# A graph-attention and feed-forward kernel: turned rows by DMA from chunk 3 on, with two sets of rows in memory and their loads ahead of x, output and s1

## What is computed

```python
def gnn(input1, input2, adj, a1, a2):
    e = input1 @ a1 + (input2 @ a2).T            # s1 of the row, s2 of the column
    e = jnp.where(e > 0, e, 0.2 * e)
    att = softmax(jnp.where(adj > 0, e, -9e15), axis=1)
    att = att * jnp.sum(adj, axis=1, keepdims=True)
    att = 0.1 * att + 0.9 * adj
    return att @ input2

x = x + gnn(layernorm(x), input2, adj, a1, a2)
x = x + layernorm(x) @ weight.T + bias
```

## Time and profile before

| | us |
|---|---|
| runs, median of 3 (lowest to highest) | 378.52 (377.69 to 378.69) |
| the profiled execution, its own time | 376.63 |
| its span, first to last instruction | 374.8 |
| PE busy in the span | 357.4 |
| PE weight loads busy | 313.6 |
| DVE busy | 311.4 |
| ACT busy | 252.9 |
| POOL busy | 146.6 |
| 4 loads of turned rows per chunk, 32 KB each: median from issue to landing | 11.8 |
| load of adj, 4 per chunk, 512 KB each: median from issue to landing | 10.9 |
| s1 into all partitions, 128 KB: median from issue to landing | 7.4 |
| x, 128 KB: median from issue to landing | 5.1 |

### The profile page before, as it was taken

The page is one execution under the profiler, slowest core; times in us unless marked ns, Lnnn a source line. Parts: engine busy times, 40 slices in busy tenths (PEclk is TensorE's granted clock), DMA queues, the critical chain, the costliest instruction groups (busy, mean ns, idle before and its releaser), DMA issues.

```text
span 374.8 us, 8950 instructions
## 1 busy us (share of the span) xinstructions
PE 357.4 (95%) x3199; PEld 313.6 (84%) x3199; DVE 311.4 (83%) x787; ACT 252.9 (67%) x616; POOL 146.6 (39%) x258
## 2 busy tenths in 40 slices
PE   5689999999999799999999999999999999999992
PEld 5578888888888688888888888888888888888881
DVE  5998989969999768879788888989687887999832
ACT  5799896697588568392947749294874929897100
POOL 4594713805262532608043260806225160703111
PEclk9999999999999999999999999999999999999998
DMA  7999959492959596694929487591958830121000
GB/s 251 202 214 202 218 110 183 78 192 45 171 119 174 117 144 136 81 202 89 204 45 181 91 145 139 96 199 42 160 118 117 160 72 2 32 26 44 30 18 30
DMA packets 34646, 45.72 MB, mean 122 GB/s; under 512 B 18084, under 2 KB 25896, under 8 KB 34600
## 3 DMA queue, kind: packets, MB, share of 16 engines
q0 software_dynamic: 9216, 33.56, 47.0%
q1 hardware_dynamic: 25384, 11.56, 16.4%
HBM read 74.84 MB, written 3.82 MB: 210 GB/s over the span
## 4 chain that ended last, share of the span: by engine, by line
PE 77%; DMA 8%; issue 5%; DVE 3%; POOL 2%; ACT 2%; SPq 1%; POOLq 0%; DVEq 0%
PE acc_u L760 23%; PE acc_v L763 23%; PE acc_y L742 21%; PE acc_v L742 4%; DMA adj_all<-adj 4%; PE acc_u L742 3%; DMA late<-block_rows 3%; PE acc_y L731 2%; PE small L725 2%; ACT steep L554 2%; DMA s_rows<-pre_s 1%; DVE plus L972 1%; POOL adj_all L409 1%; SPq L330 1%; PE acc_u L731 0%
## 5 line engine op out<-in xcount | busy, mean ns | idle before, releaser
L554 ACT ACTIVATE steep<-s_bc,steep_s 128x256 bf16<-128x256 f32 x512 | 218.2, 524 | 13.1 <-DMA s_bc<-s_rows 6.6
L763 PE MATMUL acc_v<-weights_v,minus 128*128 128x258 f16 x896 | 198.1, 272 | 0.0
L760 PE MATMUL acc_u<-weights_u,plus 128*128 128x258 f16 x896 | 198.1, 273 | 0.0
L742 PE MATMUL acc_y<-weights_y,adj_all 128*128 128x257 f16 x896 | 101.3, 273 | 0.4 <-DMA adj_all<-adj 0.4
L742 PEld LDWEIGHTS acc_y<-weights_y,adj_all 128*128 128x128 bf16 x896 | 86.8, 97 | 12.5 <-DMA adj_all<-adj 0.7
L760 PEld LDWEIGHTS acc_u<-weights_u,plus 128*128 128x128 bf16 x896 | 86.7, 97 | 12.0
L763 PEld LDWEIGHTS acc_v<-weights_v,minus 128*128 128x128 bf16 x896 | 87.1, 97 | 11.4
L972 DVE TENSOR_TENSOR plus<-adj_all,steep 128x2048 bf16<-128x2048 bf16 x64 | 80.6, 1260 | 18.5 <-ACT steep L554 18.5
L975 DVE TENSOR_TENSOR minus<-adj_all,plus 128x2048 bf16<-128x2048 bf16 x64 | 79.9, 1248 | 2.2
L568 ACT ACTIVATE num<-acc_u,ac 128x129 f32<-128x129 f32 x32 | 11.5, 364 | 87.0 <-PE acc_u L760 85.3
L453 POOL TENSOR_SCALAR post_var<-post_mv 128x2 f32<-128x2 f32 x15 | 3.3, 218 | 163.9 <-issue 133.8
(11 more groups left out here) (130 smaller groups left out, 300.1 us busy)
## 6 DMA issues: line engine op xcount, KB each, us to landing
adj_all<-adj POOLq DMA_DIRECT2D x64, 512.0 KB, 10.9
x_in<-x SPq DMA_DIRECT2D x16, 128.0 KB, 5.1
plus<-in SPq DMA_DIRECT2D x4, 512.0 KB, 5.5
out<-late SPq DMA_DIRECT2D x15, 128.0 KB, 4.6
s_bc<-s_rows SPq DMA_DIRECT2D x13, 128.0 KB, 7.4
block_rows<-late SPq DMA_DIRECT2D x13, 128.0 KB, 1.7
late<-block_rows SPq DMA_DIRECT2D x52, 32.0 KB, 11.8
s_rows<-pre_s SPq DMA_DIRECT2D x13, 1.0 KB
```

What stands on the lines that cost most here:

```text
L554: ins = nc.scalar.activation(steep[:, h, k, :].rearrange("q (t p) -> q t p", t=TILES), s1_tiles[b], ACT.Relu, bias=steep_s2[:, jt:jt + 1], ...
L742: ends[t] = nc.tensor.matmul(acc[t][:, 0:width], left[:, jt, cols(t)], right[:, jt, :, :].rearrange("p a b -> p (a b)")[:, 0:width], start ...
L760: last_u = nc.tensor.matmul(acc_u[t][:, 0:2 * WC], plus[b][:, jt, cols(t)], w_u[:, jt, :, :].rearrange("p a b -> p (a b)"), start=(jt == 0 ...
L763: last_v = nc.tensor.matmul(acc_v[t][:, 0:2 * WC], minus[b][:, jt, cols(t)], w_v[:, jt, :, :].rearrange("p a b -> p (a b)"), start=(jt == ...
```

## The change

MOVED begins with chunk 3 instead of chunk 2, so chunk 2 goes by TensorE and ACT. `block_rows` has two sets, used in turn, and the store of one chunk's blocks no longer waits for the loads of the chunk before it, but for those of the one before that. In SP's order the four loads of turned rows stand right behind the stores of blocks and s1, ahead of the load of x, the store of the output and the load of s1.

```diff
-MOVED = range(2, CHUNKS - 1)
+MOVED = range(3, CHUNKS - 1)
...
             def store_blocks(n):
                 sp.wait_ge(blocks_ready, moved(n) + 1)
-                if moved(n):
-                    sp.wait_ge(xnt_landed, 16 * BLOCKS * moved(n))
-                sp.dma_start(block_rows, x1_blocks).then_inc(blocks_stored, 16)
+                if moved(n) >= 2:
+                    sp.wait_ge(xnt_landed, 16 * BLOCKS * (moved(n) - 1))
+                sp.dma_start(block_rows[n % 2], x1_blocks).then_inc(blocks_stored, 16)
 
             def load_turned(n):
                 sp.wait_ge(blocks_stored, 16 * moved(n) + 16)
...
                     sp.dma_start(
                         xn_t[k * BLOCK:(k + 1) * BLOCK, :].rearrange("r (t a c) -> r t a c", t=TILES, c=BLOCK),
-                        block_rows.rearrange("(a r) (t k c) -> k r t a c", r=BLOCK, t=TILES, c=BLOCK)[k],
+                        block_rows[n % 2].rearrange("(a r) (t k c) -> k r t a c", r=BLOCK, t=TILES, c=BLOCK)[k],
                         ).then_inc(xnt_landed, 16)
...
                     store_blocks(c - 1)
                 if c + 2 < CHUNKS and c + 2 >= SPREAD:
                     store_s1(c + 2, b)
+                if c - 1 in MOVED:
+                    load_turned(c - 1)
                 if c + 3 < CHUNKS:
                     load_x(c + 3, 1 - b)
                 if c == 0:
...
                         store_s1(c + 2, b)
                     else:
                         load_s1(c + 2, b)
-                if c - 1 in MOVED:
-                    load_turned(c - 1)
...
-    block_rows = nc.dram_tensor("block_rows", (P, TILES * D), F32, kind="Internal").ap()
+    block_rows = nc.dram_tensor("block_rows", (2, P, TILES * D), F32, kind="Internal").ap()
```

## The result

The changed kernel took 374.41 us (median of 4 runs, 374.13 to 374.88) against 378.61 for the kernel before beside it: ratio 0.9896, 95% interval 0.9866 to 0.9927. That is 4.2 us less where 1.94 was forecast, and under the lower end of the range, 375.0. Two repeats gave the ratios 0.9917 [0.989, 0.9945] and 0.9887 [0.986, 0.9914], that is 3.1 and 4.3 us less.

A forecast was written before the change was run, and what follows sets the result against it. The prediction took PE, busy 357.4 of 374.8 us, as the bound: profiled 376.63 - 2.16 (stall) + 0.22 (two transposes) = 374.7, with the median's 1.89 excess carried over 376.6 us; range 375.0 to 378.3.

The forecast's parts named there:

- What bounds the kernel: Whole kernel: PE is busy 357.4 of 374.8 us, so only what stands on its path can move the time.
- Slot 3: PE's stretch ending with linear(2), between two linear starts: 23.65 us against a steady 21.59, an excess of 2.06 to go.
- The transposes: Two TensorE transposes for chunk 2, added to PE's path in slot 3: 0.22 us.
- the term of 2.16 us removed from PE: At linear(2) and just after: 2.06 us excess of slot 3 plus 0.10 in the next slot, removed from PE.
- linear(2) is the one place: PE from linear(2) to the end: no other gap of note; only there was turning rows by DMA too slow.
- 0.10 for what follows the stall: Slot after linear(2), 21.69 against 21.59 us: 0.10 more, for a weight load that could not run ahead.
- rival B: Other slots before linear: DMA contention stalls them too, so more is gained, 374.7 us if all 1.89 is stalls; chance 0.15.
- this offset: Median shown, 378.52 us, lies 1.89 above the profiled execution; carried over to the forecast.
- The order of the loads: SP's queue: loads ahead of x, out and s1 gain nothing on PE; margin 0.8 us in slot 4; delays cost nothing.
- Rival D: SP's queue: s1's broadcast crawls behind the loads, beyond 16.8 us masks come late, slots 4 to 11; 380.6 us; chance 0.09.
- The second set: Second set of block_rows takes a wait for the last loads off the store; it held back nobody: nothing.
- The rule on how an engine drains its rings: DMA engines: packets of 9 to 17 descriptors per ring would mean no wait at linear(2), sum +0.22; the trace was preferred.

The follow-up runs named there:

- e3: The changed kernel with chunk 2 still by DMA (new load order and two sets kept): 375.8 us, ratio 0.9941 to the kernel before.
- e15: Second timing of e3's kernel, the changed one with chunk 2 by DMA: 374.8 us, ratio 0.9908.
- e12: The kernel before, unchanged, for one more profile: profiled execution 378.62 us.
- e6: The kernel before with 14 instead of 6 warming matmuls ahead of the first product: 378.26 us, ratio 0.9998.
- e11: The kernel before with 9 useless float32 matmuls ahead of linear(2), filling the stall of slot 3: 376.9 us, ratio 0.9966.
- e2: The kernel before with only chunk 2 moved to TensorE, old load order and one set: 374.9 us, ratio 0.9917.
- e13: Second timing of e2's kernel, the kernel before with only chunk 2 by TensorE: 374.64 us, ratio 0.9903.
- e16: Third profile of e2's kernel, the kernel before with only chunk 2 by TensorE: 374.15 us, a single execution.
- e1: The kernel before, unchanged, for a second profile: ratio 0.9992, profiled execution 379.44 us.
- e4: The changed kernel with one set of block_rows in memory instead of two: 373.98 us, ratio 0.9905 to the kernel before.
- e10: The kernel before, with POOL requesting adj only when the loads of turned rows have landed: 374.15 us, ratio 0.9899.
- e9: The changed kernel with the four loads of turned rows doubled by extra ones into a spare array ahead of them: 376.27 us, ratio 0.9942.
- e8: e2's kernel (chunk 2 by TensorE, old order) with the four loads doubled by extra ones into a spare array ahead: 379.21 us, ratio 1.0015.

## Why the prediction was wrong

**What bounds the kernel: right.** PE sets the time, and the stall at linear(2) was the thing to remove.

**Slot 3: right, somewhat small.** The excess over a steady slot was taken as 2.06 from one execution; the three profiles of the kernel before have 2.06, 2.37 and 2.09, mean 2.17. The transposes cost 0.22, as two profiles (e3, e15) against three of the changed kernel show. The copy on ACT cost nothing.

**The step that failed** is the term of 2.16 us removed from PE, and with it the statement "linear(2) is the one place", both taken from one profiled execution. Over three profiles what goes is 3.44 in the mean. Two parts were missing.
The first is the clock: the stall of about 2 us in slot 3 is followed, in two of four profiles (e12, e6), by 3.4 us at half the clock, 1.7 us more. The forecast had 0.10 for what follows the stall. As a mean over the three profiles of the kernel before, slot 4's excess is 0.66, nearly all of it from e12. e11 supports the cause.
The second is rival B, which had 0.15: waits for block_rows in other slots and what follows them, 0, 0.85 and 0.98 us, mean 0.61. Its sign was there in the margins of under 1 us. Its mechanism, more contention with adj, is that of slots 10 and 11; some 0.4 of the 0.61 is in slots 13 and 14, where SP issued the loads late.
Together: 2.17 + 0.66 + 0.61 - 0.22 = 3.2 us less in the mean from linear(0) on. Of the other 1.0 of the measured 4.2, 0.8 is in the start-up, where the profiles of the kernel before have 80.84 to 82.73 (mean 81.7) and those of the changed one 80.75 to 81.09 (mean 80.9). Over all eighteen profiles linear(0) starts between 80.58 and 82.93, with no order by kernel that these few would show; the start-up's code is the same. Whether those last 0.8 us belong to the change stays open.
The median of before was 1.89 above its profiled execution. I named this offset as a sign for B and then carried it over unchanged to the forecast. The three profiles average 1.29 more than the first from linear(0) on, so as far as three profiles can tell it was such stalls and their after-effect for the most part.

**The order of the loads: nearly right that it is worth nothing.** The forecast had it harmless and useless, with the old margins thin but enough. With chunk 2 by TensorE they were enough in three profiles (e2, e13, e16), which have no waits in later slots although the loads land as late as before; the timed runs leave room for some half us. With chunk 2 by DMA in the old order such waits come in three of four (e1, e6, e12), and not in e11. With so few profiles that can in part be chance. Why a stall in slot 3 should be followed by waits seven to ten slots later I did not settle; the loads' place in the later slots looks the same in both.

**Rival D: did not decide.** s1's broadcast is later and ACT waits for it, up to 5.1 us at a time, within its idle 7.45. The loads themselves were expected to land in 3 to 8 us; the median is 3.3, but some took 13, those whose issue on SP ran into adj.

**The second set: right,** nothing (e4).

**The rule on how an engine drains its rings.** The Trainium skill ("DMA: Bandwidth & Descriptors", Queues, rings and completion order) has it drain a packet of several descriptors before it switches. The earlier trace rows gives totals over the 16 engines and not the order within one, so "record by record" is a reading of it. The changed kernel agrees with it: from 197 to 201 us queue 1 started 127 records while queue 0 started 233, where a rule that lets several small ones pass in a row would lead one to expect more small ones than large ones. The loads that fall among adj's records crawl there too, up to 13.0 us (line L330 of the changed kernel at 190 to 197 us):

```profile
DMA to landing us min/median/max: 2.7/8.7/13.0
```

## What to carry to other kernels

When PE is the bound and its slack behind a DMA is under a microsecond, one profile of it is one draw. Look at a second execution before summing stalls, above all where the median is well above the profiled time. A stall on PE of about 2 us cost nearly twice its length in e6 and e12, because the clock fell behind it; if it can't be removed, useless matmuls in its place are worth trying. And a transfer of many small records should be requested when no large one is under way: holding back adj (e10), going ahead of it, or doing without the first such transfer (e2) gave the same within 0.9 us. Where adj had ended, what made the loads late was SP's own time to issue them (e12, e9): the place in the issuing queue counts there.

## What was not expected of the hardware

The granted clock fell to half for 3.4 us after idle times of PE of 1.93 us (e12) and 2.13 (e6), and not after 1.89 (the first profile), 2.21 (e1) or 2.11 (slot 13 of e8): idle times of the same length went either way. A kernel that has more small DMAs ahead of the ones that matter (e8, 1024 records more) lost only 1.1 us in slots 4 to 12. That some 700 small records start per us once adj has run dry would explain it; no run tests it. What they cost in slots 13 and 15 was SP's time to issue them.
